# Layer 0's FP4 feed-forward block: gate-times-up products and last quantisation products given to GpSimd

## The chip, the cores and the metric

The kernel runs as one program on one core of a Trainium2 chip. The metric is the device time of one execution in microseconds (us); lower is better. The core has TensorE (PE in the profile, its weight loads PEld), VectorE (DVE), ScalarE (ACT), GpSimd (POOL) and SyncE (SP, which here only issues DMAs). Each takes its instructions in the order of the program and waits on semaphores.

## The reference, cut to what matters

Four transformer-like layers run over x, here 2 x 1024 tokens of 128 features. The change is in the feed-forward half of layer 0 alone:

```python
def fp4_quant_dequant(x):                       # blocks of 16 along the last dim
    xb = x.reshape(shape[:-1] + (shape[-1] // BLOCK, BLOCK))
    scale = jnp.max(jnp.abs(xb), axis=-1, keepdims=True) / 6.0
    scale = jnp.maximum(scale, jnp.float32(1e-12))
    xn = xb / scale
    idx = jnp.searchsorted(_MID, jnp.abs(xn))
    q = _GRID[idx] * jnp.sign(xn) * scale
    return q.reshape(shape)
def fp4_linear(x, w):
    return jnp.einsum('bsk,nk->bsn', fp4_quant_dequant(x), fp4_quant_dequant(w))
gate = fp4_linear(x, w_gate)                    # 128 -> 352
y = fp4_linear(x, w_up)                         # 128 -> 352
h = jax.nn.silu(gate) * y
return fp4_linear(h, w_down)                    # 352 -> 128
```

Its input is the layer norm of x with the layer's modulation (`layernorm(x) * (1 + cb) + sb`), and its output, times a gate, is added to x. Everything is float32.

## The kernel before, in words

Tokens lie on the partitions in 16 tiles of 128 tokens. `layer0_ffn` works on four groups g = 0 to 3 of four tiles (G = 4, NG = 4). For one group the data goes this way:

1. GpSimd modulates the normalised tiles in `gpsimd` (L1074, L1076), 128x512 elements, and counts `hm_ready`.
2. VectorE quantises them in place (`quantise_h`, through the generator `fp4`): ten instructions on 128x512, L216 (reduce to the block maxima), L219, L222, L225 (the scales, 32 per partition), L228 (times the reciprocal scale), L231, L234 (the rounding constant), L238, L242 (add it, take it away), L246 (times the scale, written to `hT`). It counts `hq`.
3. TensorE transposes the four tiles (L1098), ScalarE copies them out (L1162), TensorE multiplies each tile by the gate and the up weights (L1105, L1106), ScalarE writes silu(gate) and up to `sg` (L1166, L1167) and counts `silu`, two for a tile.
4. VectorE multiplies both halves of `sg` into `hh` (`hidden`, L1035, 128x1408) and counts `hid`. `hh` has two buffers, `sg` one.
5. VectorE quantises `hh` with the same ten lines of `fp4` on 128x1408 with 88 scales, and counts `hhq`.
6. TensorE transposes each tile in three parts (`turn_down`, L1114), ScalarE copies them out (L1174, L1175), TensorE multiplies by the down weights (`down`, L1125) and counts `down_mm`.
7. VectorE adds the result to x and takes its statistics (`x_add`, L1040, L145, L149, and L168 for the chunk before). GpSimd turns the variances into reciprocal deviations (`deviations`, L160, L162).

The order on each engine is written out by hand through the list `rounds`, round g of five having "downs" of group g-1 and "ups" of group g+1. VectorE's queue is: quantise_h(0), two chunks of normalising, quantise_h(1), hidden(0), and then in round g the quantisation of hh(g), quantise_h(g+2), x_add(g-1), hidden(g+1). All quantisations share one pair of work tiles, `tmp` and `small`. TensorE's queue in round g is turn_down of the first tile of group g-1, and then tile by tile turn_down, down and the gate and up products of group g+1. `keep_busy` (L1133) runs three idle multiplications on TensorE halfway through the quantisations of h(0) and of hh(3). Layer 1 stands behind `down` of group 3 in TensorE's queue.

Of the kernel before, what the change touches and what calls it, by code (L numbers as in the profile page):

```python
# [6 lines left out]
ALU = mybir.AluOpType  # L7
# [7 lines left out]
P = 128  # L15
# [6 lines left out]
NCH = NTOK // CH  # L22
# [53 lines left out]
def _program(nc, A, out, top):  # L76
# [30 lines left out]
    f0_tmp = sb("f0w_tmp", [P, 2, 3 * D], ctx=f0_ctx)  # L107
    f0_small = sb("f0w_small", [P, 2, 3 * XB], ctx=f0_ctx)
# [97 lines left out]

        e.wait_ge(ln_hT, NCH * nth + c + 1)

    def fp4(src, dst, rows, nb, tmp, small):

        n = nb * FB
        sc, rs = small[0:rows, 0, 0:nb], small[0:rows, 1, 0:nb]
# [30 lines left out]
        at = v_step.now()  # L243
        yield
        dv.wait_ge(*at)
        yield dv.tensor_tensor(blk(dst), blk(v), wide(sc), ALU.mult)  # L246

    def fp4_all(*args):
        *_, last = fp4(*args)
        return last  # L250

# [110 lines left out]
    sync_start()
    scalar_start()
# [619 lines left out]
    def layer0_ffn(ctx):  # L983
        G = TPC
        EARLY = (B - 1) * CPB
        NG = NT // G
        tmp = sb("f0_tmp", [P, 2, G * FI], ctx=ctx)
        small = sb("f0_small", [P, 2, G * HB], ctx=ctx)
        hm = hT[:].rearrange("p (t d) -> p t d", d=D)
        xqT = sb("f0_xqT", [P, 2, G * P], ctx=ctx)  # L990
        sg = sb("f0_sg", [P, 2, G, FI], ctx=ctx)
# [12 lines left out]

        rounds = [([g - 1] if g > 0 else [], [g + 1] if g + 1 < NG else []) for g in range(NG + 1)]

        def vector():
            dv.wait_ge(wt_tr, 1)
            dv.tensor_copy(wguT[:], ps[:, 5:7, 0:FI]).then_inc(wt, 1)
            dv.wait_ge(wt_tr, 2)  # L1010
            dv.wait_ge(gate_ready, 1)
            for b in range(B):
                for k in range(3):
                    r = FKT[k]
                    dv.tensor_tensor(wdT[0:r, b, k, :], ps[0:r, 7, k * P:(k + 1) * P],
                                     gate[0:r, 0, 1, b, :], ALU.mult).then_inc(wt, 1)

            def quantise_h(g):
                flat = hm[:, g * G:(g + 1) * G, :].rearrange("p t d -> p (t d)")
                dv.wait_ge(hm_ready, g + 1)  # L1020
                if g > 0:
                    dv.wait_ge(hq, g)
                if g >= 2:
                    dv.wait_ge(hhq, g - 1)
                for n, last in enumerate(fp4(flat, flat, P, G * XB, tmp, small)):
                    if g == 0 and n == 5:
                        half_way.append(v_step.now())
                last.then_inc(hq, 1)

            def hidden(g):  # L1030
                flat = lambda a_: a_.rearrange("p t n -> p (t n)")
                dv.wait_ge(silu, 2 * (g + 1) * G)
                if g >= 2:
                    dv.wait_ge(h_tr, (g - 1) * G)
                dv.tensor_tensor(flat(hh[:, g % 2]), flat(sg[:, 0]), flat(sg[:, 1]), ALU.mult).then_inc(hid, 1)  # L1035
# [12 lines left out]
            for g, (downs, ups) in enumerate(rounds):
                if g < NG:
                    flat = hh[:, g % 2].rearrange("p t n -> p (t n)")  # L1050
                    dv.wait_ge(hid, g + 1)
                    dv.wait_ge(hq, min(g + 2, NG))
                    for n, last in enumerate(fp4(flat, flat, P, G * HB, tmp, small)):
                        if g == NG - 1 and n == 6:
                            half_way.append(v_step.now())
                    last.then_inc(hhq, 1)
# [2051 lines left out]
```

## Time and profile before

| what | value |
| --- | --- |
| time, median of 3 runs | 1251.55 us (1249.97 to 1255.73) |
| the profiled execution | 1258.5 us, span 1257.2 us |
| PE busy | 915.5 us (73%) |
| DVE busy | 899.7 us (72%) |
| ACT busy | 578.6 us (46%) |
| POOL busy | 547.4 us (44%) |
| place of the stage | about 325 to 414 us of the span |

The shares are means over eight half-layers with different limits, so a change inside one of them has to be read in that stage's own stretch of the trace.

### The profile page before, as it was taken

The page shows a single profiled execution, that of the slowest core. Times are in us where ns is not written, and L with a number is a line of the kernel's source. Part 1 is how long each engine was busy: PE and PEld are TensorE (multiplying, and loading weights), DVE is VectorE, ACT ScalarE, POOL GpSimd, SP SyncE. Part 2 cuts the span into 40 slices and gives each one's busy share as a digit, 9 for nine tenths or more (in the row PEclk, how much of TensorE's full clock was granted, in tenths as well). Part 3 has the DMA queues.
Part 4 walks back from the last instruction along what each step waited for, and adds up shares of the span by engine and source line. Part 5 has one row for each costly group of instructions (what it writes and reads, how often), then busy time and mean ns, then how long its engine had stood idle before and what let it go on. Part 6 is the DMA issues. An engine that isn't in the chain of part 4 may idle for free.

```text
span 1257.2 us, 18690 instructions
## 1 busy us (share of the span) xinstructions
PE 915.5 (73%) x5207; PEld 533.2 (42%) x5207; DVE 899.7 (72%) x1700; ACT 578.6 (46%) x1232; POOL 547.4 (44%) x553
## 2 busy tenths in 40 slices
PE   6977787888666866678889888679893850558782
PEld 3522234333344552222223322469893530547682
DVE  6679999999999377877887871754455589972223
ACT  3478663665132443146776668334342740223232
POOL 2068995999401323201112211245534585235643
PEclk9879898999877988679998999679996775669896
DMA  8000000000000301311110100511102000011113
GB/s 294 1 1 1 1 0 1 1 1 1 1 0 1 134 1 53 98 27 27 27 28 27 27 2 2 201 62 35 39 27 78 1 0 1 9 42 36 41 33 113
DMA packets 28018, 46.32 MB, mean 37 GB/s; under 512 B 8721, under 2 KB 16409, under 8 KB 26897
## 3 DMA queue, kind: packets, MB, share of 16 engines
q1 hardware_dynamic: 22672, 34.67, 8.6%
q0 software_dynamic: 4096, 8.35, 2.2%
q10 hardware_dynamic: 1152, 2.10, 0.4%
q8 instruction: 49, 0.80, 0.3%
q14 instruction: 49, 0.39, 0.1%
HBM read 34.46 MB, written 12.58 MB: 37 GB/s over the span
## 4 chain that ended last, share of the span: by engine, by line
PE 39%; DVE 30%; issue 11%; ACT 8%; POOL 5%; DMA 3%; another core or an unknown queue 2%; SPq 1%; DVEq 0%; ACTq 0%; POOLq 0%
PE ps L2798 9%; PE ps L2807 5%; PE ps L1821 5%; PE ps L1803 4%; DVE sb_hs L756 3%; POOL sb_gs L926 3%; DVE sb_l_mxp L1935 2%; PE ps L1748 2%; DVE sb_xn L168 2%; DVE sb_stats L145 2%; ACT sb_l_rc L2228 1%; PE ps L1756 1%; ACT sb_l_pT L1878 1%; DVE ps L718 1%
## 5 line engine op out<-in xcount | busy, mean ns | idle before, releaser
L1935 DVE TENSOR_REDUCE sb_l_mxp<-ps 128x2 f32<-128x1024 f32 (+3 forms) x152 | 171.5, 1163 | 41.5 <-PE ps L1748 40.2
L926 POOL TENSOR_TENSOR sb_gs<-sb_hs,sb_xp 128x512 f32<-128x512 f32 x128 | 163.2, 1294 | 23.2 <-DVE sb_hs L756 21.1
L1878 ACT ACTIVATE sb_l_pT<-ps 128x512 f32<-128x512 f32 (+3 forms) x256 | 111.4, 521 | 76.8 <-PE ps L1803 75.7
L2798 PE MATMUL ps<-sb_hT,sb_f_shared 128*128 x936 | 127.5, 288 | 13.6 <-ACT sb_f_shared L2815 6.8
L605 PE MATMUL ps<-sb_gs,sb_ident 128*128 128x512 f32 x256 | 133.8, 605 | 1.0 <-POOL sb_gs L926 0.7
L2798 PEld LDWEIGHTS ps<-sb_hT,sb_f_shared 128*128 128x128 f32 x936 | 116.6, 200 | 22.2 <-issue 22.2
L2868 DVE SCALAR_TENSOR_TENSOR sb_f_rows<-ps,sb_f_mask,sb_f_rows 128x128 f32 x78 | 27.4, 351 | 116.6 <-PE ps L2807 57.0
L1803 PE MATMUL ps<-sb_l_qk 51*128 51x512 bf16 (+3 forms) x384 | 89.3, 335 | 19.0 <-ACT sb_l_pT L1878 7.8
L2896 POOL DMA_INDIRECT moe_y<-sb_f_rows,sb_f_rowi x64 | 63.8, 997 | 82.4 <-DVE sb_f_rows L2868 69.7
L2807 PE MATMUL ps<-sb_sw_f_out,sb_f_hid 128*128 x624 | 86.3, 283 | 14.0 <-ACT sb_f_hid L2837 9.3
L2837 ACT ACTIVATE sb_f_hid<-ps 128x512 f32<-128x512 f32 x78 | 46.5, 596 | 103.3 <-PE ps L2798 75.9
L872 ACT ACTIVATE sb_xp<-ps 128x512 f32<-128x512 f32 x96 | 57.1, 595 | 73.0 <-POOL sb_gs L926 55.0
L2891 POOL DMA_INDIRECT sb_f_inq<-moe_h,sb_f_toki x64 | 63.0, 984 | 52.1 <-PE ps L2788 18.3
L2807 PEld LDWEIGHTS ps<-sb_sw_f_out,sb_f_hid 128*128 128x128 f32 x624 | 78.6, 198 | 15.9 <-issue 15.7
L756 DVE TENSOR_TENSOR_SCAN sb_hs<-sb_dA,ps 128x512 f32<-128x512 f32 x64 | 77.0, 1203 | 0.1
L1748 PE MATMUL ps<-sb_l_qk 48*128 48x128 bf16 (+3 forms) x576 | 69.5, 300 | 8.5 <-DVE sb_l_mxp L1935 8.5
L1803 PEld LDWEIGHTS ps<-sb_l_qk 51*128 51x128 bf16 x384 | 25.6, 94 | 114.0 <-issue 107.9
L160 POOL TENSOR_SCALAR sb_rstd<-sb_meanvar 128x4 f32<-128x4 f32 x32 | 10.0, 311 | 145.7 <-DVE sb_meanvar L149 145.5
L2024 POOL TENSOR_SCALAR_AFFINE_SELECT sb_l_raw<-sb_l_raw 128x512 f32<-128x512 f32 x24 | 15.2, 635 | 132.6 <-ACT sb_l_raw L1878 132.5
L718 DVE TENSOR_TENSOR ps<-sb_mod_space,ps 128x512 f32<-128x512 f32 x96 | 64.7, 674 | 3.9 <-PE ps L571 3.9
L2024 POOL TENSOR_SCALAR_AFFINE_SELECT sb_l_pT<-sb_l_pT 128x512 f32<-128x512 f32 x40 | 25.4, 635 | 95.6 <-ACT sb_l_pT L1878 95.5
L859 ACT ACTIVATE sb_dA<-sb_dt,sb_negA 128x512 f32<-128x512 f32 x96 | 65.5, 712 | 0.8 <-DVE sb_hs L756 0.8
(394 smaller groups left out, 2046.8 us busy)
## 6 DMA issues: line engine op xcount, KB each, us to landing
sb_sw_f_in<-w_f_in SPq DMA_DIRECT2D x2, 2048.0 KB, 10.1
sb_sw_f_out<-w_f_out SPq DMA_DIRECT2D x2, 2048.0 KB, 13.1
sb_l_qk<-spill SPq DMA_DIRECT2D x112, 32.0 KB
spill<-sb_l_parts SPq DMA_DIRECT2D x12, 256.0 KB, 2.9
moe_y<-c_f_zero SPq DMA_DIRECT2D x1, 2048.0 KB, 9.8
sb_sw_f_up<-w_f_up SPq DMA_DIRECT2D x1, 2048.0 KB, 12.1
moe_h<-sb_f_rows SPq DMA_DIRECT2D x8, 256.0 KB, 5.2
sb_f_rows<-moe_y SPq DMA_DIRECT2D x8, 256.0 KB, 6.1
```

Source lines behind the costliest of these rows:

```text
L605: pe.matmul(ps[:, 4 + e * CPB + hf, :], ident[:], gs[:, p % SL, :], start=False, stop=n == DS - 1).then_inc(acc, 1)
L718: dv.tensor_tensor(ps[:, q % NB_, :], dtu[:, e, t0:t0 + CH], ps[:, q % NB_, :], ALU.mult).then_inc(inputs, 1)
L756: dv.tensor_tensor_scan(hs[:, q % SL, :], *operands, hs[:, (q - 1) % SL, CH - 1:CH] if hf else 0.0, ALU.mult, ALU.add).then_inc(scanned, 1)
L859: ac.activation(dst, dt[:, e, t0:t0 + CH], ACT.Exp, scale=negA[:, e, n:n + 1]).then_inc(decayed, 1)
L926: gp.tensor_tensor(gs[:, q % SL, :], hs[:, q % SL, :], cs[:, k % 2, hf * CH:(hf + 1) * CH], ALU.mult).then_inc(times_c, 1)
L1748: m = pe.matmul(ps[:, b0 + half, col:col + width], qs[i][rows, slot, t * P:(t + 1) * P], ks[i][rows, slot, key:key + width], start=start, ...
L1803: pe.matmul(ps[:, bank[n_sc], 0:width], ks[i][rows, h // 2, kt * P:(kt + 1) * P], qs[i][rows, h // 2, q0:q0 + width], start=True, stop=Tru ...
L1878: ac.activation(pT[e % 3][:, h, 0:width], ps[:, bank[n_bank], 0:width], ACT.Exp, scale=L2_SCALE).then_inc(exped, 1)
L1935: dv.tensor_reduce(dst, src, AX_X, ALU.max).then_inc(max_out, 1)
L2798: m = pe.matmul(ps[:, 2 * (i % 2) + n, fs], own[:, i % 2, n, fs], xr[:, bass.ds(r, 1), :], start=True, stop=True)
L2807: m = pe.matmul(ps[:, Y_BANK[i % 2], 0:D], hid[:, i % NBUF, f * P:(f + 1) * P], w_out[:, bass.ds(e, 1), f, :], start=f == 0, stop=f == FT - 1)
L2896: gp.indirect_dma_start(ysum, bass.IndirectOffsetOnAxis(ap=row_i[:, k:k + 1], axis=0), y_all[:, k, :], None, bounds_check=2 * NTOK - 1, oo ...
```

## The change: who does which product

`fp4` now ends before its last product (L246 of before), which becomes a function of its own, `fp4_back`, that takes the engine. VectorE still does it for h(0), h(1) and hh(3); GpSimd does it for h(2), h(3), hh(0), hh(1) and hh(2). `hidden` is done by VectorE for group 0 and by GpSimd for groups 1, 2 and 3. There are two sets of `tmp` and `small`: h(0), hh(0), hh(1) and hh(2) use set 0, h(1), h(2), h(3) and hh(3) use set 1. GpSimd's `deviations(2, c)` stand behind the products of their round. The weights' quantisations keep all on VectorE.

```diff
-    def fp4(src, dst, rows, nb, tmp, small):
+    def fp4(src, rows, nb, tmp, small):
...
-        dv.wait_ge(*at)
-        yield dv.tensor_tensor(blk(dst), blk(v), wide(sc), ALU.mult)
+    def fp4_back(e, at, dst, rows, nb, tmp, small):
+
+        e.wait_ge(*at)
+        blk = lambda a: a.rearrange("p (k i) -> p k i", i=FB)
+        sc = small[0:rows, 0, 0:nb].unsqueeze(2).to_broadcast([rows, nb, FB])
+        return e.tensor_tensor(blk(dst), blk(tmp[0:rows, 0, 0:nb * FB]), sc, ALU.mult)
...
-        tmp = sb("f0_tmp", [P, 2, G * FI], ctx=ctx)
-        small = sb("f0_small", [P, 2, G * HB], ctx=ctx)
+        tmp = [sb(f"f0_tmp{z}", [P, 2, G * FI], ctx=ctx) for z in range(2)]
+        small = [sb(f"f0_small{z}", [P, 2, G * HB], ctx=ctx) for z in range(2)]
...
+        def z_h(g):
+
+            return 0 if g == 0 else 1
+
+        def z_hidden(g):
+
+            return 1 if g == NG - 1 else 0
+
+        def free_hidden(g):
+
+            if g == 0:
+                return hq, 1
+            return (hq, NG) if z_hidden(g) else (hhq, g)
+
+        def hidden(e, g):
+            flat = lambda a_: a_.rearrange("p t n -> p (t n)")
+            e.wait_ge(silu, 2 * (g + 1) * G)
+            if g >= 2:
+                e.wait_ge(h_tr, (g - 1) * G)
+            e.tensor_tensor(flat_hh(g), flat(sg[:, 0]), flat(sg[:, 1]), ALU.mult).then_inc(hid, 1)
...
             def quantise_h(g):
-                flat = hm[:, g * G:(g + 1) * G, :].rearrange("p t d -> p (t d)")
+                z = z_h(g)
                 dv.wait_ge(hm_ready, g + 1)
-                if g > 0:
+                if g >= 2:
                     dv.wait_ge(hq, g)
-                if g >= 2:
-                    dv.wait_ge(hhq, g - 1)
...
+            def quantise_hh(g):
+                z = z_hidden(g)
+                dv.wait_ge(hid, g + 1)
+                dv.wait_ge(*(free_hidden(g)))
...
             quantise_h(0)
+            scaled_h(dv, 0)
             for c in range(EARLY, NCH):
                 normalise(1, c)
             quantise_h(1)
-            hidden(0)
+            scaled_h(dv, 1)
+            hidden(dv, 0)
             for g, (downs, ups) in enumerate(rounds):
                 if g < NG:
...
+                    quantise_hh(g)
+                if g == NG - 1:
+                    dv.wait_ge(hhq, g)
+                    scaled_hh(dv, g)
                 if g + 2 < NG:
                     quantise_h(g + 2)
                 for d in downs:
                     x_add(d)
-                for u_ in ups:
-                    hidden(u_)
...
         def gpsimd():
...
-            for c in range(NCH):
-                deviations(2, c)
+            for g, (downs, ups) in enumerate(rounds):
+                for u_ in ups:
+                    hidden(gp, u_)
+                if g < NG - 1:
+                    scaled_hh(gp, g)
+                if g + 2 < NG:
+                    scaled_h(gp, g + 2)
+                for d in downs:
+                    deviations(2, d)
```

`scaled_h` and `scaled_hh` call `fp4_back` for h(g) and hh(g) with their set and count `hq` and `hhq`. TensorE's and ScalarE's queues are as before.

## Rows read from the trace of the kernel before

**Rows 1.** Windows: stretch, length, busy us of PE, PEld, DVE, ACT, POOL, PEclk, DMA share, GB/s.

```profile
341.60:360.00 18.40, 10.53 (x32) 6.59 (x32) 17.61 (x23) 4.96 (x13) 0.00 (x0) 0.74 0.00 0
380.30:396.00 15.70, 14.05 (x66) 10.35 (x66) 15.29 (x24) 5.99 (x18) 3.28 (x4) 0.76 0.01 2
396.00:398.00 2.00, 2.00 (x19) 1.84 (x17) 1.97 (x3) 0.82 (x4) 0.53 (x1) 1.00 0.00 0
404.00:406.00 2.00, 1.84 (x3) 1.17 (x4) 1.93 (x3) 0.00 (x0) 0.00 (x0) 0.50 0.00 0
```

**Rows 2.** Timeline of DVE (start us, length us, instruction): the stage's quantisations.

```profile
343.21 1.62 DVE L216 TENSOR_REDUCE sb_f_small<-sb_f_hh 128x88 f32<-128x1408 f32 x1
344.86 0.20 DVE L219 TENSOR_SCALAR sb_f_small<-sb_f_small 128x88 f32<-128x88 f32 x1
...
351.26 1.62 DVE L242 TENSOR_TENSOR sb_f_tmp<-sb_f_tmp 128x1408 f32<-128x1408 f32 x1
...
354.67 0.69 DVE L216 TENSOR_REDUCE sb_f_small<-sb_hT 128x32 f32<-128x512 f32 x1
355.39 0.18 DVE L219 TENSOR_SCALAR sb_f_small<-sb_f_small 128x32 f32<-128x32 f32 x1
...
359.31 0.69 DVE L246 TENSOR_TENSOR sb_hT<-sb_f_tmp,sb_f_small 128x512 f32<-128x512 f32 x1
...
396.01 1.61 DVE L1035 TENSOR_TENSOR sb_f_hh<-sb_f_sg 128x1408 f32<-128x1408 f32 x1
...
407.37 1.62 DVE L246 TENSOR_TENSOR sb_f_hh<-sb_f_tmp,sb_f_small 128x1408 f32<-128x1408 f32 x1
```

**Rows 3.** The chain that ended last: the step behind the last quantisation.

```profile
409.05 0.87 PE ps L1114 x6
```

**Rows 4.** Timeline of DVE, quantise_h(1), while POOL modulates groups 2 and 3.

```profile
335.88 1.70 DVE L228 TENSOR_TENSOR sb_f_tmp<-sb_hT,sb_f_small 128x512 f32<-128x512 f32 x1
337.62 1.38 DVE L231 TENSOR_SCALAR sb_f_tmp<-sb_f_tmp 128x512 uint32<-128x512 uint32 x1
```

**Rows 5.** Timeline of POOL, from the modulation to layer 1.

```profile
335.77 1.27 POOL L1074 TENSOR_TENSOR sb_hT<-sb_xn,sb_mod 128x512 f32<-128x512 f32 x1
337.12 1.59 POOL L1076 TENSOR_TENSOR sb_hT<-sb_hT,sb_mod 128x512 f32<-128x512 f32 x1
380.38 1.51 POOL L160 TENSOR_SCALAR sb_rstd<-sb_meanvar 128x4 f32<-128x4 f32 x1 [41.67 <-DVE sb_meanvar L149]
...
395.49 1.04 POOL L162 TENSOR_TENSOR sb_rstd<-sb_rstd,sb_half 128x4 f32<-128x4 f32 x1
...
424.48 2.35 POOL L1420 TENSOR_TENSOR sb_x<-sb_x,sb_sw_l_in 128x1024 f32<-128x1024 f32 x1
```

**Rows 6.** Timeline of ACT: the last write to `sg` of groups 1, 2 and 3.

```profile
350.12 0.46 ACT L1167 ACTIVATE sb_f_sg<-ps 128x352 f32<-128x352 f32 x1
...
372.59 0.46 ACT L1167 ACTIVATE sb_f_sg<-ps 128x352 f32<-128x352 f32 x1
...
393.01 0.46 ACT L1167 ACTIVATE sb_f_sg<-ps 128x352 f32<-128x352 f32 x1
```

**Rows 7.** Timeline of PE: turn_down, down and keep_busy.

```profile
354.60 1.54 PE L1114 MATMUL ps<-sb_ident,sb_f_hh 128*128 128x128 f32 x6 [4.87 <-DVE sb_f_hh L246]
356.13 1.65 PE L1125 MATMUL ps<-sb_f_wdT,sb_f_hqT 128*128 128x128 f32 x6
...
379.02 1.65 PE L1125 MATMUL ps<-sb_f_wdT,sb_f_hqT 128*128 128x128 f32 x6 [5.19 <-DVE sb_x L1040]
...
393.23 0.87 PE L1114 MATMUL ps<-sb_ident,sb_f_hh 128*128 128x128 f32 x6 [0.61 <-DVE sb_f_hh L246]
...
396.53 1.73 PE L1125 MATMUL ps<-sb_f_wdT,sb_f_hqT 128*128 128x128 f32 x12
404.16 3.86 PE L1133 MATMUL ps<-sb_f_wguT,sb_ident 128*128 128x352 f32 x6 [5.90 <-DVE sb_f_tmp L234]
```

**Rows 8.** All of line 2416: GpSimd's slowest product, min/median/max ns.

```profile
L2416 POOL TENSOR_TENSOR sb_l_pr<-sb_l_sc,sb_l_v x5: 2778/2784/2792, 1028.8 to 1058.0; 128x1024 f32<-128x1024 f32 x5
```

More of the change, by code:

```diff
@@ L242, in fp4, with fp4_all @@
         dv.tensor_tensor(v, v, e, ALU.subtract).then_inc(*v_step.up())
-        at = v_step.now()
         yield
-        dv.wait_ge(*at)
-        yield dv.tensor_tensor(blk(dst), blk(v), wide(sc), ALU.mult)
-    def fp4_all(*args):
-        *_, last = fp4(*args)
-        return last
+    def fp4_back(e, at, dst, rows, nb, tmp, small):
[3 more added lines that the diff above has]
+        return e.tensor_tensor(blk(dst), blk(tmp[0:rows, 0, 0:nb * FB]), sc, ALU.mult)
+    def fp4_all(part, rows, nb, tmp, small):
+        for _ in fp4(part, rows, nb, tmp, small):
+            pass
+        return fp4_back(dv, v_step.now(), part, rows, nb, tmp, small)
     mod_mm, mod_act, mod_silb = sem("mod_mm"), sem("mod_act"), sem("mod_silb")
@@ L356, in quantise_weight @@
             part = w["w_f0_gu"][:, 3 * k:3 * k + 3, :].rearrange("p k d -> p (k d)")
-            fp4_all(part, part, P, 3 * XB, f0_tmp, f0_small).then_inc(f0_quant, 1)
+            fp4_all(part, P, 3 * XB, f0_tmp, f0_small).then_inc(f0_quant, 1)
         else:
             wdn = w["w_f0_dn"]
-            fp4_all(wdn[:], wdn[:], P, HB, f0_tmp, f0_small).then_inc(f0_quant, 1)
+            fp4_all(wdn[:], P, HB, f0_tmp, f0_small).then_inc(f0_quant, 1)
     sync_start()
@@ L1005, in layer0_ffn, with scaled_h, scaled_hh @@
         rounds = [([g - 1] if g > 0 else [], [g + 1] if g + 1 < NG else []) for g in range(NG + 1)]
+        h_whole, hh_whole = {}, {}
+        flat_h = lambda g: hm[:, g * G:(g + 1) * G, :].rearrange("p t d -> p (t d)")
+        flat_hh = lambda g: hh[:, g % 2].rearrange("p t n -> p (t n)")
+        def z_h(g):
[12 more added lines that the diff above has]
+            e.tensor_tensor(flat_hh(g), flat(sg[:, 0]), flat(sg[:, 1]), ALU.mult).then_inc(hid, 1)
+        def scaled_h(e, g):
+            z = z_h(g)
+            fp4_back(e, h_whole[g], flat_h(g), P, G * XB, tmp[z], small[z]).then_inc(hq, 1)
+        def scaled_hh(e, g):
+            z = z_hidden(g)
+            fp4_back(e, hh_whole[g], flat_hh(g), P, G * HB, tmp[z], small[z]).then_inc(hhq, 1)
         def vector():
@@ L1018, in quantise_h @@
             def quantise_h(g):
-                flat = hm[:, g * G:(g + 1) * G, :].rearrange("p t d -> p (t d)")
+                z = z_h(g)
                 dv.wait_ge(hm_ready, g + 1)
-                if g > 0:
+                if g >= 2:
                     dv.wait_ge(hq, g)
-                if g >= 2:
-                    dv.wait_ge(hhq, g - 1)
-                for n, last in enumerate(fp4(flat, flat, P, G * XB, tmp, small)):
+                for n, _ in enumerate(fp4(flat_h(g), P, G * XB, tmp[z], small[z])):
                     if g == 0 and n == 5:
                         half_way.append(v_step.now())
[L1028 to L1035, printed above, removed]
+                h_whole[g] = v_step.now()
+            def quantise_hh(g):
+                z = z_hidden(g)
+                dv.wait_ge(hid, g + 1)
+                dv.wait_ge(*(free_hidden(g)))
+                for n, _ in enumerate(fp4(flat_hh(g), P, G * HB, tmp[z], small[z])):
+                    if g == NG - 1 and n == 6:
+                        half_way.append(v_step.now())
+                hh_whole[g] = v_step.now()
             def x_add(g):
@@ L1046, in vector @@
             quantise_h(1)
-            hidden(0)
+            scaled_h(dv, 1)
+            hidden(dv, 0)
             for g, (downs, ups) in enumerate(rounds):
                 if g < NG:
[L1050 to L1056, printed above, removed]
+                    quantise_hh(g)
+                if g == NG - 1:
+                    dv.wait_ge(hhq, g)
+                    scaled_hh(dv, g)
                 if g + 2 < NG:
```

## The prediction

> **What bounds the kernel now.** I read the windows of the stage first. VectorE is busy for 17.61 of 18.40 us in the first round and for 15.29 of 15.70 us in the third, TensorE for 10.53 and 14.05 us, GpSimd for 0 and 3.28 us [rows 1]. So the stage runs at VectorE's pace, and GpSimd has time to spare. The chain that ended last says the same: it goes through VectorE's quantisations, and its last product (407.37 us + 1.62 = 408.99) releases TensorE's `turn_down` of group 3 at 409.05 [rows 2, 3]. Layer 1 stands behind that work in TensorE's queue, and nothing ahead of it depends on a clock of its own. So a microsecond by which this product moves is a microsecond at the end, and the question is only when it ends.
>
> The timelines then say what an engine does when VectorE and GpSimd are both at work. While GpSimd modulated (335.77 to 337.04), VectorE's L228, which takes 0.69 us by itself (L246 of the same shape and kinds of operands), took 1.70 us: it ended at 337.58, 0.54 us after GpSimd's instruction [rows 2, 4, 5]. GpSimd's next one, in turn, took 1.59 instead of 1.27 us and ended 1.13 us after L228 did, and L231 then ended 0.29 us after that [rows 4, 5]. At 380.38 a GpSimd instruction on 128x4 elements took 1.51 us beside VectorE's product of two SBUF tiles [rows 5]. So a GpSimd instruction and a VectorE product of two SBUF tiles, or a tensor_scalar, don't run side by side here: one waits for the whole other, and then ends its own time, less about 0.15 us of start, later.
>
> **The change part by part.** VectorE loses three gate-times-up products and three last products of 128x1408 (1.62 us each) and two last products of 128x512 (0.69 us each) [rows 2]: 6 x 1.62 + 2 x 0.69 = 11.1 us. That is the gain if nothing else binds.
>
> GpSimd's price: 512 elements take 1.27 us, 1024 take 2.35 us [rows 5], so 2.11 ns an element, and 1408 take 1.27 + 896 x 2.11 ns = 3.16 us. It gets 6 x 3.16 + 2 x 1.27 = 21.5 us. The nearest row for a bad pattern is 2.78 us for 1024 [rows 8], 3.83 us for 1408. Three of the six have a scale that repeats within 16 elements, which no row shows on GpSimd. I take 3.16, since the modulation's operand repeats too [rows 5], and keep 3.83 for the range.
>
> Now the schedule, walked with these lengths; an instruction that was held ends 0.15 us less than its own length behind the one that held it. Handing over between engines costs about 0.08 us.
>
> Up to 351.2 us all is as before. The second set of work tiles removes a wait for VectorE's own last product, which cost nothing since VectorE had no gap there.
>
> *hidden(1).* `sg` of group 1 is whole at 350.58 [rows 6]. VectorE is in L238 until just ahead of 351.26. GpSimd gets in behind it and ends at 351.25 + 3.16 - 0.14 = 354.27. L242 of hh(0) is held and ends at 355.74; before 352.88 [rows 2].
>
> *Last product of hh(0).* GpSimd, 355.8 to 358.98. VectorE starts quantise_h(2): the reduction (0.69 us) runs beside it, L219 is held until 359.03. From L219's end to L242's end it was 359.28 - 355.57 = 3.71 us [rows 2], so L242 ends at 362.74, before 359.28. GpSimd's last product of h(2) then ends at 364.09, before 360.00: TensorE gets h(2) 4.1 us later. Whichever engine is let in first at 351.25 changes this little, since it is the same two instructions in a row.
>
> *Round 1.* VectorE quantises hh(1) from 362.77 (before 361.58); reduction to L242 is 352.88 - 343.21 = 9.67 us [rows 2], so it is ready for its last product at 372.4, and quantise_h(3) takes until 377.1 (4.61 us, 354.67 to 359.28). But GpSimd's queue has hidden(2) ahead of that product. `sg` of group 2 was whole 13.05 us after h(2) (373.05 - 360.00) [rows 2, 6], so now at 377.14. hidden(2) ends at 380.4, and the product of hh(1), ready since 372.4, at 383.5. VectorE needs it both for set 0 and through hid, and has nothing but x_add(0) to do: it begins hh(2) at 383.5. (Before it began at about 381.8, where the product that held L160 until 381.89 had ended [rows 5].)
>
> *Round 2.* TensorE's queue has `turn_down` of group 1 ahead of h(3). With two cold tiles `down` follows `turn_down` by 356.13 - 354.60 = 1.53 us, so it starts at 385.1, before 379.02 [rows 7]: 6.1 us later. `sg` of group 3 was whole 14.45 us behind that row (393.47) [rows 6, 7], so now at 399.6. TensorE has been at work longer by then and may be at its full clock sooner, for which I take off 0.4 us: 399.2. hidden(3) ends at 402.4; before it ended at 397.62 [rows 2]. The product of hh(2) again stands behind it and ends at 405.55. VectorE does hh(3)'s reduction beside it and L219 ends at 405.6. From there to L242 is 352.88 - 345.06 = 7.82 us, to 413.4, and VectorE's own last product ends at 415.1. Before: 408.99. That is +6.1 us.
>
> *keep_busy.* `down` of group 2 was over 5.0 us behind its `turn_down` (393.23 to 398.26) at full clock [rows 1, 7]. Now it starts at 405.6 behind an idle stretch of about 7 us. After 5.90 us of idle TensorE ran at the lower level, 0.50 [rows 1, 7]. So 5.0 to 10.1 us, until 410.6 to 415.7, and only then keep_busy, 3.86 us cold [rows 7] or half of it: until 412.5 to 419.6. The middle is 416, the product comes at 415.1. I take +0.6 us and keep 0 and +4.5.
>
> Sum: 6.1 + 0.6 = +6.7 us, for the profiled execution 1258.5 + 6.7 = 1265.2. That execution lies 0.6% above the median of the runs shown, so I add the sum to the median: 1251.55 + 6.7 = 1258.3 us. A measurement of this kernel tells about 0.5% (6.3 us) from no change, so the forecast is just past that.
>
> At one place a rule would raise the sum. The row: the power L162, two SBUF operands on GpSimd, ran from 395.49 to 396.53, and VectorE's L1035 beside it took 1.61 us, not held [rows 2, 5]. The Trainium skill, SBUF — State Buffer, section "Who interferes with whom", has the shared ports as an exclusive lock kept for the whole instruction, by which L1035 would have ended some 0.4 us later. By the row the deviations of group 1, which now fall beside L219 to L228 of hh(3), cost nothing; by the rule up to 1.0 us more, 1259.3. For the long products row and rule agree.
>
> **The rivals.**
>
> *No exclusion for these shapes.* For: nothing in the trace has GpSimd at 128x1408. Against: [rows 4, 5]. Then L242 of hh(0) ends at 352.9, hidden(1) at 353.8, hh(0) is whole at 357.0, h(2) at 358.9 (-1.1), `sg` 2 at 372.0, hidden(2) and hh(1) at 378.3, `down` of group 1 at 379.95 (+0.9), `sg` 3 at 394.4, hidden(3) at 397.6, as before; hh(3) is whole at 408.9. So -0.1 us, 1251.5: not slower. Even here the 11.1 us don't come, because hh(1) waits behind hidden(2). It decides if L242 of hh(0) ends by 353.5.
>
> *keep_busy stands in the way.* For: the idle stretch ahead of group 2's `down`. Against: the dense work may bring the clock back within it. The end of `turn_down` would shift by 8 to 10.5 us: about 1261.
>
> *Repeating scales are slow on GpSimd.* 3.83 for 3.16 us on hh(0), hh(1), hh(2), all three on the path: +2.0, so +8.7, 1260.3.
>
> *The full lock for the power*: +7.7, as worked out above.
>
> *TensorE's clock returns sooner.* With a mean of 0.76 between two levels of 0.5 and 1, 0.48 of the 15.7 us of the third round ran at half speed, 7.5 us [rows 1]. Each microsecond less of idle before it, or of slow start, gives back half of it, 3.8 us at most in round 2 and about as much in round 1. A part of it gives +2 to +5.5: 1255.5. All of it, together with no exclusion, would be -7.7, 1243.9; that is the only way I see to a time that is faster.
>
> **How the numbers follow.** Forecast, +5.5 to +8: 0.42, of which 0.25 above 6.3. keep_busy 0.15, the power 0.07, slow scales 0.07, clock sooner 0.18, no exclusion 0.07, and 0.04 for the faster end. Slower: 0.25 + 0.15 + 0.07 + 0.07 = 0.54. Same: 0.17 + 0.18 + 0.07 = 0.42. Faster 0.04. The range reaches from no exclusion (1251.5, rounded down to 1251) to keep_busy at its worst (+10.5 to +11.5, 1263). The forecast's own range is 1257 to 1259.5.
>
> **What would show it.** L242 of hh(0) at about 4.5 us and ended at 355.7. L219 of quantise_h(2) near 2.5 us. GpSimd's products at 3.1 to 3.2 us. A gap in VectorE of 4 us or so ahead of hh(2), which begins at 383.5, and another ahead of hh(3)'s reduction at 402.4. The last product at 415.1, and keep_busy later than half way. Where the reduction of hh(2) begins before 382, GpSimd's queue is not the limit and the prediction is wrong; where `turn_down` of group 3 starts much behind the last product, the keep_busy term was too small.

## The result and the profile after

| | before | after |
| --- | --- | --- |
| median, 20 runs each | 1255.62 us (1249.97 to 1261.84) | 1262.19 us (1254.6 to 1272.74) |
| ratio | | 1.0064, 95% interval 1.0046 to 1.0081 |
| profiled execution, span | 1257.2 us | 1260.0 us |
| PE, DVE, ACT, POOL busy | 915.5, 899.7, 578.6, 547.4 us | 918.1, 897.0, 580.3, 568.1 us |

The change makes the kernel slower by 0.64%, 8.0 us (5.8 to 10.2). The forecast was a sum of +6.7 us, 0.54%. As a time, 1258.3 us, it was set on the median of three runs, 1251.55 us. With 20 runs the kernel before has 1255.62 us, so the forecast time is only 0.21% above it, and the measured change is 0.64%. The sum agrees with the profiles to about a microsecond; the time that was built on it is 3.9 us too low, because its base was 4.1 us too low.

I read each profile by one measure, the stage: from the reduction of h(0) to layer 1's first product on TensorE (L1292 before, L1334 after), cut where the last product of hh(3) ends. L250 is now the last product of every quantisation.

```profile
326.21 0.67 DVE L216 TENSOR_REDUCE sb_f_small<-sb_hT 128x32 f32<-128x512 f32 x1
...
353.27 0.68 DVE L216 TENSOR_REDUCE sb_f_small<-sb_hT 128x32 f32<-128x512 f32 x1
353.98 2.42 DVE L219 TENSOR_SCALAR sb_f_small<-sb_f_small 128x32 f32<-128x32 f32 x1
356.44 0.35 DVE L222 RECIPROCAL sb_f_small<-sb_f_small 128x32 f32<-128x32 f32 x1
356.82 2.12 DVE L225 TENSOR_SCALAR sb_f_small<-sb_f_small 128x32 f32<-128x32 f32 x1
...
370.00 1.62 DVE L242 TENSOR_TENSOR sb_f_tmp<-sb_f_tmp 128x1408 f32<-128x1408 f32 x1
...
381.93 1.62 DVE L216 TENSOR_REDUCE sb_f_small<-sb_f_hh 128x88 f32<-128x1408 f32 x1 [3.86 <-POOL sb_f_hh L250]
...
397.02 6.20 DVE L168 TENSOR_SCALAR sb_xn<-sb_x,sb_meanvar,sb_rstd 128x128 f32<-128x128 f32 x4
403.14 1.60 DVE L216 TENSOR_REDUCE sb_f_small<-sb_f_hh 128x88 f32<-128x1408 f32 x1
404.78 0.21 DVE L219 TENSOR_SCALAR sb_f_small<-sb_f_small 128x88 f32<-128x88 f32 x1
...
412.90 1.62 DVE L250 TENSOR_TENSOR sb_f_hh<-sb_f_tmp,sb_f_small 128x1408 f32<-128x1408 f32 x1
```

This is VectorE's timeline (start us, length us). GpSimd's, of the same kernel:

```profile
352.48 3.88 POOL L1035 TENSOR_TENSOR sb_f_hh<-sb_f_sg 128x1408 f32<-128x1408 f32 x1 [13.29 <-ACT sb_f_sg L1209]
356.33 2.58 POOL L250 TENSOR_TENSOR sb_f_hh<-sb_f_tmp,sb_f_small 128x1408 f32<-128x1408 f32 x1
362.12 1.06 POOL L250 TENSOR_TENSOR sb_hT<-sb_f_tmp,sb_f_small 128x512 f32<-128x512 f32 x1 [3.22 <-DVE sb_f_tmp L242]
376.13 3.15 POOL L1035 TENSOR_TENSOR sb_f_hh<-sb_f_sg 128x1408 f32<-128x1408 f32 x1 [12.94 <-ACT sb_f_sg L1209]
379.24 2.58 POOL L250 TENSOR_TENSOR sb_f_hh<-sb_f_tmp,sb_f_small 128x1408 f32<-128x1408 f32 x1
381.79 1.05 POOL L250 TENSOR_TENSOR sb_hT<-sb_f_tmp,sb_f_small 128x512 f32<-128x512 f32 x1
...
397.17 3.16 POOL L1035 TENSOR_TENSOR sb_f_hh<-sb_f_sg 128x1408 f32<-128x1408 f32 x1 [13.02 <-ACT sb_f_sg L1209]
400.30 2.58 POOL L250 TENSOR_TENSOR sb_f_hh<-sb_f_tmp,sb_f_small 128x1408 f32<-128x1408 f32 x1
```

And TensorE's and ScalarE's:

```profile
381.88 1.54 PE L1156 MATMUL ps<-sb_ident,sb_f_hh 128*128 128x128 f32 x6 [6.68 <-POOL sb_f_hh L250]
...
402.93 1.54 PE L1156 MATMUL ps<-sb_ident,sb_f_hh 128*128 128x128 f32 x6 [6.69 <-POOL sb_f_hh L250]
...
409.68 1.95 PE L1175 MATMUL ps<-sb_f_wguT,sb_ident 128*128 128x352 f32 x6
414.58 1.54 PE L1156 MATMUL ps<-sb_ident,sb_f_hh 128*128 128x128 f32 x6 [2.94 <-DVE sb_f_hh L250]
...
420.65 0.39 PE L1334 MATMUL ps<-sb_sw_l_ffn 128*128 128x128 f32 x2
```

```profile
351.95 0.46 ACT L1209 ACTIVATE sb_f_sg<-ps 128x352 f32<-128x352 f32 x1
...
375.59 0.46 ACT L1209 ACTIVATE sb_f_sg<-ps 128x352 f32<-128x352 f32 x1
...
396.64 0.46 ACT L1209 ACTIVATE sb_f_sg<-ps 128x352 f32<-128x352 f32 x1
```

Four things are to be seen in them, each against the groups ahead of the prediction.

*The exclusion.* L219, 0.18 us by itself [rows 2], takes 2.42 us beside hidden(1) and ends 0.04 us after it (356.36). L225 takes 2.12 us beside the last product of hh(0), and the reciprocal between them (0.35 us) goes through untouched.

*The queue.* L242 of hh(1) ends at 371.62, so its last product could start. GpSimd starts it at 379.24, behind hidden(2), which waited for ScalarE until 376.05. VectorE is idle for 3.86 us ahead of hh(2). In the kernel before it had no such gap. (The last 2.6 us of the gap are the queue's; until 379.28 hh(2) itself wasn't there, since hidden(2) makes it.)

*A third wait.* Four small tensor_scalars, L168, take 6.20 us (1.08 alone) while hidden(3) and the last product of hh(2) run back to back on GpSimd. hh(3) begins at 403.14, though hidden(3) ended at 400.33. The four one by one, min/median/max ns:

```profile
L168 DVE TENSOR_SCALAR sb_xn<-sb_x,sb_meanvar,sb_rstd x4: 315/1477/3170, 397.0 to 402.9; 128x128 f32<-128x128 f32 x4
```

The longest, 3.17 us, was held by hidden(3) and ended 0.1 us behind it, at 400.42. The next took 2.62 us, held by the last product of hh(2); the other two took about 0.3 us each (the median, 1477 ns, lies midway between the second and the third). So each of GpSimd's two instructions held one of the four.

*The tail.* keep_busy ends at 411.63, TensorE is then idle for 2.94 us, and `turn_down` of group 3 takes 1.54 us where it took 0.87 [rows 3]. The granted clock was 1.00 from 412 to 414 and 0.51 from 416 to 418; a stretch at the lower level is called cold below.

The stage took 420.65 - 326.21 = 94.44 us, before 413.92 - 325.75 = 88.17. Of these +6.3 us, +5.1 stand ahead of the last product's end (88.31 against 83.24) and +1.2 in the tail (6.13 against 4.93).

### The profile page after: what moved, and what is told of

It is laid out like the page before. It is cut to its first block, busy times and chain, and to the rows that moved or that the text cites. A ratio compares the mean times of both kernels' runs of the same rounds, so it can differ in the third digit from the quotient of the medians.

```text
span 1260.0 us, 18690 instructions
## 1 busy us (share of the span) xinstructions
PE 918.1 (73%) x5207; PEld 536.1 (43%) x5207; DVE 897.0 (71%) x1692; ACT 580.3 (46%) x1232; POOL 568.1 (45%) x561
## 4 chain that ended last, share of the span: by engine, by line
PE 43%; DVE 28%; issue 11%; ACT 8%; POOL 5%; DMA 3%; SPq 1%; another core or an unknown queue 1%; DVEq 0%; ACTq 0%; POOLq 0%
PE ps L2840 9%; PE ps L2849 5%; PE ps L1863 5%; PE ps L1845 4%; DVE sb_hs L761 3%; POOL sb_gs L931 3%; DVE sb_l_mxp L1977 2%; PE ps L1790 2%; DVE sb_xn L168 2%; DVE sb_stats L145 2%; ACT sb_l_rc L2270 1%; PE ps L1798 1%; ACT sb_l_pT L1920 1%; DVE ps L723 1%; PE ps L489 1%
## 5 line engine op out<-in xcount | busy, mean ns | idle before, releaser
L2066 POOL TENSOR_SCALAR_AFFINE_SELECT sb_l_raw<-sb_l_raw 128x512 f32<-128x512 f32 x24 | 15.3, 637 | 133.1 <-ACT sb_l_raw L1920 133.0
L1920 ACT ACTIVATE sb_l_raw<-ps 128x512 f32<-128x512 f32 (+2 forms) x128 | 52.6, 476 | 29.5 <-PE ps L1845 29.4
```

The source lines that it names most:

```text
L1920: ac.activation(pT[e % 3][:, h, 0:width], ps[:, bank[n_bank], 0:width], ACT.Exp, scale=L2_SCALE).then_inc(exped, 1)
```

## The experiments

All kernels of one table, from their profiles. "Last product" is the end of hh(3)'s last product and "stage" layer 1's first product, both counted from the stage's start. The tail is what lies between the two. "Rest" is the span behind the stage, whose work is the same in all. Each row is one profile; where the last column is empty, the kernel was timed only once.

| kernel | last product | tail | stage | rest | ratio to before, 95% |
| --- | --- | --- | --- | --- | --- |
| before | 83.24 | 4.93 | 88.17 | 843.3 | 1 |
| before_again | 83.22 | 4.93 | 88.15 | 842.0 | |
| after | 88.31 | 6.13 | 94.44 | 839.4 | 1.0064 (1.0046 to 1.0081) |
| after_again | 89.29 | 6.18 | 95.47 | 846.7 | |
| sets_only | 82.96 | 6.31 | 89.27 | 844.0 | 1.0002 (0.9979 to 1.0025) |
| hidden_only | 86.31 | 7.45 | 93.76 | 842.9 | 1.0034 (1.0017 to 1.0051) |
| scaled_only | 80.82 | 6.52 | 87.34 | 839.2 | 0.9996 (0.9972 to 1.0019) |
| queue_order | 85.57 | 6.49 | 92.06 | 848.3 | 1.0054 (1.0033 to 1.0075) |
| normalise_later | 87.52 | 4.93 | 92.45 | 845.4 | 1.0038 (1.0018 to 1.0058) |
| busy_longer | 89.29 | 4.92 | 94.21 | 850.2 | 1.0062 (1.0039 to 1.0085) |
| three_mended | 82.98 | 4.93 | 87.91 | 846.3 | 1.0012 (0.9988 to 1.0037) |
| scaled_busy | 80.78 | 4.93 | 85.71 | 846.7 | 1.0002 (0.9978 to 1.0026) |
| idle_products | 100.59 | 6.56 | 107.15 | 842.6 | 1.0155 (1.0136 to 1.0174) |
| idle_writes | 91.42 | 4.93 | 96.35 | 844.8 | |

The rest spreads from 839 to 850 us with no order in it. So a single span can't show 2 us of this stage, and neither can a ratio known to 0.2%. The stage's own length can: it repeats to 0.02 us in the kernel before and to 1.0 us in the changed one, whose VectorE waits for TensorE's products. Differences under 1 us between kernels of the second kind are not shown by it.

### Is it exclusion? idle_products and idle_writes

Each adds to the kernel before, on a tile of its own, work that nobody waits for until the stage's end, at the events of the changed kernel. In idle_writes the product is replaced by two `gp.memset(idle[:, 2, 0:n], 0.0)`. Both clear their tile first, behind the modulation.

```diff
-            for c in range(NCH):
-                deviations(2, c)
...
+            def idle_product(n):
+                gp.tensor_tensor(idle[:, 2, 0:n], idle[:, 0, 0:n], idle[:, 1, 0:n], ALU.mult).then_inc(*idle_at.up())
...
+            for g, (downs, ups) in enumerate(rounds):
+                for u_ in ups:
+                    gp.wait_ge(silu, 2 * (u_ + 1) * G)
+                    idle_product(G * FI)
+                if g < NG - 1:
+                    gp.wait_ge(*hh_at[g])
+                    idle_product(G * FI)
+                if g + 2 < NG:
+                    gp.wait_ge(*h_at[g + 2])
+                    idle_product(G * D)
...
```

> The kernel before, with eight products on GpSimd added on a tile of its own, of the same six 128x1408 and two 128x512 sizes and released at the same events as in the changed kernel; nothing waits for them until the stage's end, and no work is taken from VectorE. Theory (a GpSimd product and VectorE's two-input products and tensor_scalars exclude each other): each long one costs VectorE 2.5 to 3 us, stage 103 to 107 us. Rival (they run side by side but for starts): stage 88 to 89 us.

> The kernel before with idle work on GpSimd at the same eight events, two memsets instead of each product, so that GpSimd only writes SBUF. In the run with idle products a memset of 128x2816 (339.49 to 341.93) held VectorE's line 231, a tensor_scalar, until 342.22. Theory (a write alone excludes tensor_scalar but not products of two tiles): lines 219, 231, 234 are held where memsets fall on them, 228, 238, 242, 246 keep 0.69 and 1.62 us; stage 92 to 100 us. Rival (every GpSimd instruction excludes both): 238 and 242 are held too, stage 103 us or more.

Measured: idle_products has a stage of 107.15 us, 0.15 above its range and 19.0 more than before, and the timed runs agree: 1.0155 is 19.5 us. idle_writes has 96.35, within its range. The timelines of VectorE and GpSimd in idle_products:

```profile
354.48 4.55 DVE L242 TENSOR_TENSOR sb_f_tmp<-sb_f_tmp 128x1408 f32<-128x1408 f32 x1
```

```profile
354.40 3.15 POOL L1090 TENSOR_TENSOR sb_f_idle<-sb_f_idle 128x1408 f32<-128x1408 f32 x1 [12.47 <-ACT sb_f_sg L1194]
```

and in idle_writes:

```profile
357.04 1.62 DVE L246 TENSOR_TENSOR sb_f_hh<-sb_f_tmp,sb_f_small 128x1408 f32<-128x1408 f32 x1
...
359.52 0.54 DVE L219 TENSOR_SCALAR sb_f_small<-sb_f_small 128x32 f32<-128x32 f32 x1
...
360.48 0.91 DVE L225 TENSOR_SCALAR sb_f_small<-sb_f_small 128x32 f32<-128x32 f32 x1
```

```profile
356.09 5.26 POOL L1091 MEMSET sb_f_idle<- 128x1408 f32 x4 [13.25 <-ACT sb_f_sg L1195]
```

GpSimd's product, which reads two tiles and writes one, holds VectorE's L242 for nearly its whole length: 4.55 us instead of 1.62. Four memsets leave the product L246 at its 1.62 us, but stretch the tensor_scalars L219 and L225 from 0.18 to 0.54 and 0.91. So the theory stands, and the rival "side by side" falls. Of the last product's 17.35 us of delay in idle_products, 2.4 are the first memset's (L231 took 3.76 us there, 1.38 before [rows 4]). That leaves 15 us for eight products of together about 21 us, and the stretched instructions of VectorE add up to just these: L242 2.9, L219 2.0 and 2.0, the gate-times-up product 1.1, L225 2.6, the four L168 4.3. So these products cost VectorE some 70% of their own length, where a product that is taken from it saves it 51% (1.62 of 3.16) or 63% (1.62 of 2.58). The 70% hold for these places only: what a product costs depends on what VectorE is at beside it.

The Trainium skill, SBUF — State Buffer, section "Who interferes with whom", says the same: a VectorE instruction with two SBUF inputs contends with a GpSimd instruction that reads SBUF and not with one that only writes it, and a tensor_scalar in its two-port mode contends with GpSimd. These two runs agree with it.

### Which part? hidden_only, scaled_only, sets_only

Against the changed kernel, hidden_only:

```diff
                 if g < NG:
                     quantise_hh(g)
-                if g == NG - 1:
-                    dv.wait_ge(hhq, g)
+                if g < NG:
+                    if g:
+                        dv.wait_ge(hhq, g)
                     scaled_hh(dv, g)
                 if g + 2 < NG:
                     quantise_h(g + 2)
+                    scaled_h(dv, g + 2)
...
                 for u_ in ups:
                     hidden(gp, u_)
-                if g < NG - 1:
-                    scaled_hh(gp, g)
-                if g + 2 < NG:
-                    scaled_h(gp, g + 2)
```

and scaled_only:

```diff
                 for d in downs:
                     x_add(d)
+                for u_ in ups:
+                    hidden(dv, u_)
...
-                for u_ in ups:
-                    hidden(gp, u_)
```

sets_only has both edits: all products on VectorE, two sets of tiles.

> The changed kernel with only the products of gate and up on GpSimd (groups 1 to 3); all last products of the quantisations back on VectorE. Stage length is counted from the reduction of h(0) to layer 1's first product: 88.2 us before, 94.4 us changed. Theory (the product of gate and up on GpSimd stands in the path and holds VectorE by the shared port): stage 90 to 92 us, so most of the loss is here. Rival (the loss comes from GpSimd's queue, where a last product waits behind hidden): no last product is in that queue now, stage 86 to 88 us.

> The changed kernel with only the five last products of the quantisations on GpSimd; gate times up back on VectorE at the end of each round. Theory (loss from hidden in GpSimd's queue): each last product starts the moment its tile is ready, VectorE is held about 2 us for each of the long ones and saves 1.6; stage 86.5 to 87.5 us, 1 us or so below before. Rival (holding by the shared port is the main loss): stage 90 us or more.

> The changed kernel with all products on VectorE, so that only the two sets of work tiles and the order of the waits are left. Theory (the second set is of no account by itself, since VectorE had no gap at these waits): stage 88.2 us, tail 4.9 to 6.5. Rival (the tiles' places or waits cost): stage 90 us or more.

Measured: hidden_only 93.76 us, 1.8 above its range. Its tail is the slowest of all, 7.45 us: TensorE's granted clock was 0.50 from 406 to 418. With the tail of before it would be at 91.2, inside the range. The last product is at 86.31, 3.1 later than before. The rival, that a queue alone is at fault, falls. scaled_only hits its range: last product 80.82, which is 2.4 us sooner than before, of which a tail of 6.52 takes back 1.6. sets_only, 1.1 above the 88.2 expected, is the kernel before in all but the tail.

VectorE's timelines say why the one part loses and the other gains. In hidden_only:

```profile
351.88 4.45 DVE L242 TENSOR_TENSOR sb_f_tmp<-sb_f_tmp 128x1408 f32<-128x1408 f32 x1
...
375.78 2.62 DVE L225 TENSOR_SCALAR sb_f_small<-sb_f_small 128x32 f32<-128x32 f32 x1
...
397.42 3.95 DVE L168 TENSOR_SCALAR sb_xn<-sb_x,sb_meanvar,sb_rstd 128x128 f32<-128x128 f32 x4
```

and in scaled_only:

```profile
353.55 2.07 DVE L219 TENSOR_SCALAR sb_f_small<-sb_f_small 128x32 f32<-128x32 f32 x1
...
371.20 2.07 DVE L219 TENSOR_SCALAR sb_f_small<-sb_f_small 128x32 f32<-128x32 f32 x1
...
391.95 1.68 DVE L168 TENSOR_SCALAR sb_xn<-sb_x,sb_meanvar,sb_rstd 128x128 f32<-128x128 f32 x4
```

Each of the three gate-times-up products holds VectorE for 2.4 to 2.9 us and saves it 1.62: 8.1 us against 4.9. The three long last products hold it for 1.9, 1.9 and 0.6 us, since a reduction or x_add's first steps run beside them, and the short ones not at all: 4.4 us against 6.2 saved.

The two parts don't add: +3.1 and -2.4 make +0.7, the change has +5.1. What is missing, 4.4 us, exists only with both on GpSimd. The waits of the next section are its likely place.

### Where do the parts meet? queue_order, normalise_later, busy_longer, three_mended

queue_order puts hidden last in GpSimd's round:

```diff
             for g, (downs, ups) in enumerate(rounds):
-                for u_ in ups:
-                    hidden(gp, u_)
                 if g < NG - 1:
                     scaled_hh(gp, g)
                 if g + 2 < NG:
                     scaled_h(gp, g + 2)
+                for u_ in ups:
+                    hidden(gp, u_)
```

normalise_later has `close_chunk(1, g, held=(1,))`, by which x_add(1) doesn't normalise and x_add(2) normalises two chunks. busy_longer has `keep_busy(half_way[1], 8)`, with the count in place of three. three_mended has normalise_later's edit, `keep_busy(half_way[1], 5)`, and queue_order's in rounds 1 and 2 alone: hidden(1) stays ahead in round 0.

> The changed kernel, GpSimd's queue in each round in the order last product of hh(g), last product of h(g+2), hidden(g+1), instead of hidden first. Theory (in rounds 1 and 2 the last product of hh waits for the silu of the next group, 4 and 7 us, and TensorE's next group starts that much late): hidden(1) comes 2 us later, down of group 1 starts near 376 instead of 382, gate and up of group 3 3 to 4 us sooner; stage 90.5 to 92 us. Rival (the order is of no account, port and length of the instructions decide): 94 us as the changed kernel.

> The changed kernel with the normalising of chunk 0 (line 168, after x_add(1)) moved behind x_add(2). In the changed kernel these four instructions took 6.2 us instead of 1.1, beside GpSimd's hidden(3) and last product of hh(2), and hh(3) began at 403.1 though its product was there at 400.3. Theory (VectorE's tensor_scalar stands in the path, held over both GpSimd instructions): hh(3)'s reduction begins at hidden(3)'s end and runs beside the last product of hh(2), 2 us come back, stage 92.2 to 92.7 us. Rival (VectorE would be held by GpSimd anyway at its next instruction): stage 94.4 us.

> The changed kernel with eight idle multiplications instead of three in the second keep_busy. In the changed kernel keep_busy ran from 409.7 to 411.6 us, TensorE was idle for 2.9 us, the granted clock was 0.63 and 0.51 in the windows from 414 to 418, and the tail from the last product of hh(3) to layer 1's first product took 6.1 us against 4.9 before. Theory (the idle stretch costs the clock, and this is a term of its own, about 1.2 us): eight last until 414.6, tail 4.9 to 5.2 us, stage 93.2 to 93.5. Rival (the tail's clock falls whatever TensorE does just ahead): tail 6 us or more, stage 94.4 or more.

> The changed kernel with the same work on GpSimd and three waits taken away: in rounds 1 and 2 hidden comes last in GpSimd's queue, behind the products that were ready before it; the normalising of chunk 0 comes behind x_add(2); the second keep_busy has five multiplications. Theory (these three are the whole loss): hh(2) starts about as in the changed kernel, hh(3) 4 us sooner, the last product of hh(3) ends 83 to 84.5 us after the stage's start (before 83.2, changed 88.3), stage 88 to 89.5 us. Rival (exclusion costs more than VectorE saves, whatever the order): last product at 86 us or later, stage 91 us or more.

Measured: queue_order 92.06, a bare 0.1 above its range. hidden(1) came late in it (VectorE idle for 4.28 us ahead of hh(1)), but the last product of hh(1) began 5.4 us sooner in the stage than in the changed kernel, and the last product of hh(3) ended 2.7 us sooner. The rival, that the order is of no account, falls. normalise_later 92.45, in the expected range, but only 0.8 of the 2.0 us lie ahead of the last product, and 1.2 in the tail. Since the silu of group 3 came 1.3 us later there than in the changed kernel, the clean measure is from hidden(3)'s start to the last product's end: 411.28 - 395.99 = 15.29 against 414.52 - 397.17 = 17.35, 2.1 us less. The tail's 1.2 go with TensorE's idle stretch ahead of it, which was 0.77 us there and 2.94 in the changed kernel. busy_longer: the tail is 4.92 as expected, but `sg` of group 3 was whole 1.0 us later and the last product came 1.0 later with it, as in after_again, so the stage is 94.21 instead of 93.2 to 93.5. As a whole busy_longer isn't faster than the changed kernel (1.0062 against 1.0064). three_mended: last product 82.98, stage 87.91, with the same eight products on GpSimd. Its timelines of VectorE and GpSimd:

```profile
382.00 1.62 DVE L218 TENSOR_REDUCE sb_f_small<-sb_f_hh 128x88 f32<-128x1408 f32 x1 [2.36 <-POOL sb_f_hh L1037]
...
397.49 1.62 DVE L218 TENSOR_REDUCE sb_f_small<-sb_f_hh 128x88 f32<-128x1408 f32 x1 [3.91 <-POOL sb_f_hh L1037]
...
407.27 1.62 DVE L252 TENSOR_TENSOR sb_f_hh<-sb_f_tmp,sb_f_small 128x1408 f32<-128x1408 f32 x1
```

```profile
371.39 2.59 POOL L252 TENSOR_TENSOR sb_f_hh<-sb_f_tmp,sb_f_small 128x1408 f32<-128x1408 f32 x1 [8.53 <-DVE sb_f_tmp L244]
...
378.81 3.15 POOL L1037 TENSOR_TENSOR sb_f_hh<-sb_f_sg 128x1408 f32<-128x1408 f32 x1
...
391.75 2.59 POOL L252 TENSOR_TENSOR sb_f_hh<-sb_f_tmp,sb_f_small 128x1408 f32<-128x1408 f32 x1 [8.47 <-DVE sb_f_tmp L244]
394.29 3.17 POOL L1037 TENSOR_TENSOR sb_f_hh<-sb_f_sg 128x1408 f32<-128x1408 f32 x1
```

Counted from the stage's start, the last product of hh(1) now begins 7.6 us sooner than in the changed kernel (371.39 - 325.91 against 379.24 - 326.21), and hh(3)'s reduction 5.4 us sooner. hh(2) is no sooner: its hidden, whose inputs were there by 375.7, still waits its turn on GpSimd until 378.81. Against normalise_later, which differs in the queue's order and in idle multiplications that VectorE doesn't wait for, that product ends 4.5 us sooner, or 3.3 if the 1.3 us of its late silu are taken off: this is what the order costs. The three waits account for the whole loss, and the rival, that exclusion eats it all whatever the order, falls: without them the exchange is even.

One comparison is missing. three_mended also has four L168 (1.08 us alone) behind the last product that the kernel before has ahead of it, and the kernel before was not run with that move alone. Since its VectorE has no gap there, the move would give it about 1 us, by estimate, and against such a kernel the exchange would lose as much.

### Is the tail fixed? before_again, after_again, scaled_busy

> The kernel before, unchanged, for a second profile. Theory (the order fixes all but the clock's phase): last product of hh(3) at 83.0 to 83.5 us of the stage; tail 4.9 or 6.3 us, since two kernels with the same order there had the one and the other. Rival (the stage is fixed to 0.3 us): 83.2 and 4.9.

> The changed kernel, unchanged, for a second profile. Theory (here VectorE waits for the silu that TensorE's clock sets, so the place of the last product moves with the clock's phase): last product at 87.3 to 89.5 us of the stage, tail 4.9 to 6.3. Rival (fixed): 88.3 and 6.1.

> The version with only the last products on GpSimd (stage 87.3 us, tail 6.5), with five idle multiplications instead of three in the second keep_busy. Theory (last products alone are a gain of 2.4 us up to hh(3)'s last product, of which a cold tail took back 1.6): tail 4.9 to 5.3 us, stage 85.8 to 86.3, time 0.1 to 0.2% below before. Rival (the tail's clock isn't set by this): tail 6.5, stage 87.3, time as before.

Measured: before_again has 83.22 and 4.93, the kernel before again. But sets_only, with the same order, had 6.31. TensorE's timelines of before (its keep_busy is in [rows 7]), of sets_only and of idle_writes:

```profile
409.05 0.87 PE L1114 MATMUL ps<-sb_ident,sb_f_hh 128*128 128x128 f32 x6 [1.03 <-DVE sb_f_hh L246]
```

```profile
405.24 3.86 PE L1173 MATMUL ps<-sb_f_wguT,sb_ident 128*128 128x352 f32 x6 [5.90 <-DVE sb_f_tmp L234]
410.20 1.54 PE L1154 MATMUL ps<-sb_ident,sb_f_hh 128*128 128x128 f32 x6 [1.10 <-DVE sb_f_hh L250]
```

```profile
418.98 0.87 PE L1141 MATMUL ps<-sb_ident,sb_f_hh 128*128 128x128 f32 x6 [1.14 <-DVE sb_f_hh L246]
```

In the first two keep_busy takes 3.86 us, and the idle time behind it is 1.03 us in the kernel before and 1.10 in sets_only. The one's clock is at 0.93 in the window 408 to 410 and 1.00 after it, the other's at 0.50 until 412. The length of the idle time isn't what tells them apart: in idle_writes it was 1.14 us, and `turn_down` took 0.87 and the tail 4.93. What does stays open, so a tail of 6.3 us isn't the change's by itself.

In the changed kernel the tail was cold both times (6.13, 6.18), with an idle stretch of 2.9 us; with eight or five idle multiplications that reach up to the last product it was 4.92 or 4.93 in all three kernels that had them. after_again had its last product at 89.29, in the expected range. scaled_busy has 85.71, 0.1 under its range, the shortest stage here and 2.5 us under before. Its time, 1.0002 (0.9978 to 1.0026), doesn't show them: the 0.1 to 0.2% that were expected aren't seen, and whether it beats the kernel before stays open.

## Why the prediction was right or wrong

**The direction and the sum.** Slower, by +6.7 us forecast; the stage's two profiles gave +6.3 and +7.3, the timed runs +8.0 (5.8 to 10.2).

**The step that failed in the time: the base.** The prediction added the sum "to the median: 1251.55 + 6.7 = 1258.3 us", and that median was of three runs. Twenty runs have 1255.62, 4.1 us more. On it the same sum gives 1262.3 us, and 1262.19 was measured.

The sum is also a better hit than its terms:

| checkpoint, us of the trace | forecast | measured |
| --- | --- | --- |
| L242 of hh(0) ends | 355.7 | 353.35 |
| last product of hh(0) ends | 358.98 | 358.91 |
| h(2) whole | 364.09 | 363.18 |
| sg of group 2 whole | 377.14 | 376.05 |
| last product of hh(1) ends | 383.5 | 381.82 |
| sg of group 3 whole | 399.2 | 397.10 |
| last product of hh(2) ends | 405.55 | 402.88 |
| L219 of hh(3) ends | 405.6 | 404.99 |
| last product of hh(3) ends | 415.1 | 414.52 |

(The stage began 0.46 us later in the trace of after.)

**What held.** The exclusion: a held tensor_scalar ends about its own length, less 0.15 us, behind GpSimd's instruction, and L219 ended 0.04 us behind. The queue: hidden(2) and hidden(3) ahead of products that were ready, each seen, and taken away in three_mended. The gap ahead of hh(2), 3.86 us for "4 us or so". That nothing comes of the 11.1 us.

**A sign that misfired.** The prediction called itself wrong where hh(2)'s reduction begins before 382. It began at 381.93, and GpSimd's queue was the limit all the same: the profile has it released by the last product of hh(1), which stood behind hidden(2). The sign was set too close, with last products of 3.16 us.

**GpSimd's price.** hidden took 3.15 us, as worked out (3.16). The last products took 2.58, not 3.16, and 1.06 for 512 elements, not 1.27. A scale that repeats over 16 neighbours makes GpSimd faster; I had kept a slower one (3.83) for the range. That is some 0.6 us too much in each of three steps on the path, -1.7, and 0.2 for h(2).

**hidden(1) against L242.** The forecast had GpSimd let in ahead of L242. `sg` of group 1 was whole at 352.41, 1.4 us later in the stage than before [rows 6], and hidden(1) came behind L242, which kept its 1.62 us where the prediction had 4.5. As argued, this changed little at the product's end. But it changed what was held: hidden(1) held L219 (2.42 us, near the 2.5 forecast for the other product, by luck), and the last product of hh(0) only L225, 0.6 us further on in the chain. So h(2) came 0.6 us sooner than by the walk.

**The step that failed in the walk: x_add(1).** The walk put nothing against it and let hh(3)'s reduction begin as hidden(3) ended. But x_add(1) came only at 395.09, when `down` of group 1, itself late, was done, and GpSimd had two products back to back beside its L168, a tensor_scalar that is held like the others. normalise_later prices it at 2.1 us. A row for this was there: the four L168 beside layer 1's GpSimd product.

```profile
417.60 2.13 DVE L168 TENSOR_SCALAR sb_xn<-sb_x,sb_meanvar,sb_rstd 128x128 f32<-128x128 f32 x4 [0.47 <-POOL sb_rstd L162]
```

Four of them take 1.08 us alone.

**The step that failed in the tail: keep_busy.** I added 0.6 us because it would come too late, and gave the same mechanism 0.15 as a rival at 1261. `down` of group 2 took 6.75 us (402.93 to 409.68), keep_busy ran at full clock and was over 2.9 us before it was needed. What came was the reverse, a clock that was lower behind the idle stretch, +1.2 us. The sign of the term was right and its size half of what came, by luck: the reason was wrong.

**The rivals.** No exclusion is refuted by idle_products. The full lock for the power would have held L219 to L228 of hh(3). In the changed kernel L162 (403.16 to 404.20) fell beside the reduction, so it couldn't cost anything by either reading. That the power holds nothing is shown by normalise_later, where it runs beside VectorE's tensor_scalar L227 and product L230 (L225 and L228 of the other kernels):

```profile
401.97 1.04 POOL L162 TENSOR_TENSOR sb_rstd<-sb_rstd,sb_half 128x4 f32<-128x4 f32 x1
```

```profile
402.52 0.20 DVE L227 TENSOR_SCALAR sb_f_small<-sb_f_small 128x88 f32<-128x88 f32 x1
402.76 1.63 DVE L230 TENSOR_TENSOR sb_f_tmp<-sb_f_hh,sb_f_small 128x1408 f32<-128x1408 f32 x1
```

L162 runs until 403.01, L227 keeps its 0.20 us and L230 its 1.63. By the rule of the Trainium skill, SBUF — State Buffer, section "Who interferes with whom", L227 would have ended behind 403.01 and L230 would have begun there. The measurement decides: L227 ended at 402.72 and L230 began at 402.76. TensorE's clock did return sooner in round 2: from hh(1) whole to `sg` of group 3 it took 15.3 us, 0.8 less than a plain shift (0.4 had been taken off).

**The account of the walk.** Counted from the same start, its end was 1.0 us too late: 1.7 and 0.2 for GpSimd's last products, 0.6 for what was held beside hh(0), 0.6 for `sg` that came sooner (0.2 in round 1, 0.4 in round 2), less the 2.1 of x_add(1). With the tail's 0.6 too little this makes +6.3 of +6.7. That errors of this size nearly cancel is luck.

## What to carry to other kernels

Before work goes to GpSimd, count three prices: its own length, what it holds of VectorE, and what stands behind it in its queue. The second depends on what VectorE does just then: 0.6 to 1.9 us for a last product of 2.58 us in scaled_only, which was a gain in the stage, and 2.4 to 2.9 us for a gate-times-up product in hidden_only, which was a loss. Order that queue by when inputs are ready, and look for rows of small tensor_scalars of VectorE beside two GpSimd instructions in a row: such a row waits for both. And a forecast that stands on three runs inherits their error, here 4 us of base against a sum of 7.

## What the runs showed of the hardware

- GpSimd's product of 128x1408 takes 3.15 us with two plain operands and 2.58 us with a factor repeated 16 times.
- Beside two GpSimd products that follow each other, each held one of four small tensor_scalars (3.17 and 2.62 us for 0.3), and the four took 6.20 us for 1.08.
- Beside GpSimd's products, a reduction (0.68 us) and a reciprocal (0.35 us) of VectorE kept their lengths. Beside its power on 128x4, so did a tensor_scalar (0.20 us) and a product of two tiles (1.63 us).
- GpSimd's memset holds VectorE's tensor_scalar, not its product of two tiles.
- Behind the same three idle multiplications TensorE's clock was at its upper level behind 1.03 and 1.14 us of idle time and at its lower level behind 1.10: the idle time alone didn't decide.
